# Adjacency pieces loaded on a third DMA queue (GpSimd's), with the start of the four-layer graph kernel rearranged

## The reference

```python
x = _layernorm(x + L0(x, adj, W, b))
x = _layernorm(x + L1(x, t, adj, B, W1, b1, W2, b2))
x = _layernorm(x + L2(x, adj, weight, bias))
x = _layernorm(x + L3(x, adj, kernel, bias))
# L0: relu([X, (adj @ X + X) / (degree + 1)] @ W + b), rows scaled to length 1
# L1: tanh([X, t] @ W1 + b1) @ W2 + b2 + adj @ XB - degree * XB,  XB = X @ B.T
# L2: per row the last 100 neighbours, weighted by powers of 0.5 (a cumulative
#     count along the row gives each one's place), times (X @ weight), + bias
# L3: adj @ expmap(X), then logmap, @ kernel + bias
```

## Time and profile before

| what | us |
|---|---|
| median of three runs (169.04 to 169.3) | 169.18 |
| the profiled execution | 167.48 |
| its span, first to last instruction | 165.2 |
| PE, DVE, ACT, POOL busy | 128.9, 107.6, 69.5, 42.8 |
| granted TensorE clock, mean over the span | 0.968 |

### The profile page before, as it was taken

One profiled execution on the slowest core, in us unless ns is written; L12 is line 12 of the kernel. 1 busy time (PEld: TensorE's weight loads), 2 busy tenths in 40 slices (PEclk: granted clock), 3 DMA queues, 4 the chain that ended last, 5 costly groups with the idle time before them and its releaser, 6 DMA issues.

```text
span 165.2 us, 2074 instructions
## 1 busy us (share of the span) xinstructions
PE 128.9 (78%) x728; PEld 67.7 (41%) x728; DVE 107.6 (65%) x240; ACT 69.5 (42%) x138; POOL 42.8 (26%) x50
## 2 busy tenths in 40 slices
PE   0018869957998899899999899999999899992000
PEld 0007753511443245143533555677447644572000
DVE  0589987789999999995176110622623888538861
ACT  0034201448566666754378547512113320257440
POOL 0000000102430143114344000433412552713290
PEclk9999999999999999999999999999999999999755
DMA  6999999999999995000000000000000000000006
GB/s 131 257 304 350 318 300 354 272 206 287 346 347 255 289 215 124 0 0 0 4 0 0 0 0 0 4 0 0 0 4 0 0 2 0 0 4 0 0 0 127
DMA packets 13945, 18.59 MB, mean 112 GB/s; under 512 B 5360, under 2 KB 5616, under 8 KB 13936
## 3 DMA queue, kind: packets, MB, share of 16 engines
q1 hardware_dynamic: 7728, 9.68, 22.2%
q10 hardware_dynamic: 6208, 8.78, 19.2%
HBM read 17.93 MB, written 0.52 MB: 112 GB/s over the span
## 4 chain that ended last, share of the span: by engine, by line
PE 45%; DVE 25%; DMA 13%; POOL 5%; issue 4%; ACT 4%; POOLq 1%; ACTq 0%; DVEq 0%
PE psS L737 15%; DMA WT<-adj 10%; PE psN L737 5%; PE psC L737 5%; DVE AT L494 4%; DVE AT L495 4%; DMA X<-x 3%; PE psC L804 3%; PE psC L806 3%; PE psX L813 2%; POOL root L272 2%; POOL nroot L291 2%; ACT WT L365 2%; PE psX L763 1%; PE psH L783 1%
## 5 line engine op out<-in xcount | busy, mean ns | idle before, releaser
L365 ACT ACTIVATE WT<-psC 128x512 int16<-128x512 f32 x64 | 36.9, 596 | 13.0 <-PE psC L806 9.8
L737 PE MATMUL psS<-AT,XP 128*128 128x512 bf16 x128 | 35.0, 390 | 0.9 <-DVE XP L500 0.9
L272 POOL TENSOR_TENSOR root<-var,power 128x4 f32<-128x4 f32 (+1 forms) x16 | 18.7, 1170 | 44.2 <-DVE var L546 19.5
L804 PE MATMUL psC<-AT,cb 128*128 128x512 bf16 x56 | 21.4, 383 | 4.5 <-ACT WT L365 4.5
L806 PE MATMUL psC<-AT,cb 128*128 128x512 bf16 x64 | 24.2, 379 | 0.0
L737 PEld LDWEIGHTS psS<-AT,XP 128*128 128x128 f16 x128 | 11.9, 100 | 17.0 <-issue 3.7
L763 PE MATMUL psX<-cb,XP 128*128 128x128 bf16 x32 | 4.0, 264 | 12.7 <-DVE XP L632 11.9
L494 DVE STREAM_TRANSPOSE AT<-stage 128x1024 bf16<-128x1024 bf16 x10 | 13.2, 1318 | 0.8 <-DMA stage<-adj 0.7
L804 PEld LDWEIGHTS psC<-AT,cb 128*128 128x128 bf16 x56 | 5.6, 101 | 18.6 <-ACT WT L365 16.0
L495 DVE STREAM_TRANSPOSE AT<-stage 128x1024 bf16<-128x1024 bf16 x10 | 12.7, 1270 | 0.0
L285 POOL TENSOR_TENSOR XB<-X,weights 128x256 f32<-128x256 f32 x12 | 9.6, 808 | 9.6 <-DVE X L551 9.6
(11 more groups left out here) (143 smaller groups left out, 223.3 us busy)
## 6 DMA issues: line engine op xcount, KB each, us to landing
stage<-adj ACTq DMA_DIRECT2D x20, 256.0 KB, 11.3
stage<-adj SPq DMA_DIRECT2D x20, 256.0 KB, 12.3
WT<-adj SPq DMA_DIRECT2D x12, 256.0 KB, 14.7
WT<-adj ACTq DMA_DIRECT2D x12, 256.0 KB, 14.0
out<-X SPq DMA_DIRECT2D x6, 64.0 KB, 1.9
weights<-weights_packed SPq DMA_DIRECT2D x1, 353.5 KB, 15.8
X<-x SPq DMA_DIRECT2D x2, 128.0 KB, 3.1
X<-x ACTq DMA_DIRECT2D x2, 128.0 KB, 4.0
```

The costliest lines, as they stand in the source:

```text
L272: nc.gpsimd.tensor_tensor(root[:, e, 0:n], var[:, e, 0:n], power[:, 0:n, 0:NR], ALU.pow).then_inc(root_ready, 1)
L365: nc.scalar.activation(WT[:, e, chain_block(bank, k)], psC[bank][:], ACT.Relu).then_inc(chain_taken, 1)
L737: ins = nc.tensor.matmul(bank, XP[:, l % 2, c], matrix, start=(c == 0), stop=last)
L804: nc.tensor.matmul(acc, C("past"), AT[:, c + 1, e], start=False, stop=False, skip_group_check=True)
```

## The change

X was loaded ahead of piece 0; now piece 0 comes first on both queues. DVE transposes it before it looks at X. The high half of layer 0's `XP` is made by ACT (`split_high`), and so is the copy of the own parts (`take_z`); POOL adds the bias (`add_bias`). The own parts get a PSUM bank each (`z_bank`). PE counts and sums chunk 0 in two halves (`count_half`, `sum_half`), the first after pieces 0 and 1, and makes the own parts between the halves. The upper quarters of pieces 8 to 15 are issued by POOL's queue, with semaphores of their own. DVE's orders, the chain's and layer 1's are rewritten. The core of the diff:

```diff
-        CHAIN_IN_SUMS = (0, 11, 27, 42)
-        CHAIN_LOOP = 56
+        CHAIN_IN_SUMS = (0, 10, 27, 38)
+        CHAIN_LOOP = 46
+        def chain_in_sums(e):
+            return range(CHAIN_IN_SUMS[e], min(CHAIN_IN_SUMS[e] + NB // 2, NB * e))
+        def chain_after_sums(e):
+            return range(chain_in_sums(e).stop, CHAIN_IN_SUMS[e + 1])
...
# sync: load_lower(0), X, constants, own weights, load_lower(1..3), weights, load_lower(4..15)
# gpsimd
+            def load_upper(m):
+                pool.wait_ge(transposed, m - 8 + 1 if m < 12 else m - 6 + 1)
+                for q in range(NQ // 2, NQ):
+                    nc.gpsimd.dma_start(slot(slot_of(m))[QD * q:QD * (q + 1)], ad[m, q]
+                                        ).then_inc(pool_filled[slot_of(m)], 16)
+            def add_bias(e):
+                pool.wait_ge(z_taken, e + 1)
+                nc.gpsimd.tensor_tensor(Z[:, chunk(e)], Z[:, chunk(e)], per_feature(W("b0")), ALU.add
+                                        ).then_inc(z_biased, 1)
...
+            pool.wait_ge(own_weights_loaded, 16)
+            for e in range(NE):
+                load_upper(ALL_SLOTS + e)
+                add_bias(e)
             pool.wait_ge(consts_loaded, 16)
-            for e in range(NE - 1):
+            for e in range(NE - 2):
                 weigh(e)
-                if e >= 1:
-                    residual(1, e - 1)
+                if e == 0:
+                    load_upper(12)
                 l2_root(e)
+                if e == 0:
+                    load_upper(13)
                 var_root(0, e)
                 diagonals(e)
+                if e == 0:
+                    load_upper(14)
+                    load_upper(15)
...
# scalar
+            def split_high():
+                act.wait_ge(inverse_ready, 1)
+                nc.scalar.activation(XP[:, 0, :, 0:D], X[:], ACT.Copy, scale=xs[:, 4:5]).then_inc(high_ready, 1)
+            load_upper(0)
             for q in range(NQ // 2, NQ):
                 act.dma_start(X[QD * q:QD * (q + 1)], xd[q]).then_inc(x_loaded, 16)
-            for m in range(NR):
+            for m in range(1, 6):
                 load_upper(m)
+            split_high()
+            take_xt(0, 0)
+            load_upper(6)
+            take_xt(0, 1)
+            load_upper(7)
+            take_z(0)
+            take_xt(0, 2)
+            take_z(1)
+            take_xt(0, 3)
+            take_z(2)
+            take_z(3)
...
# vector
+            transposes(0)
             # x_loaded; largest value and mean of X
+            transposes(1)
             # scale, inverse; XB; low half of XP
+            for m in range(2, 6):
+                transposes(m)
+            take_degrees(0)
+            transposes(6)
+            activate0(0)
+            transposes(7)
+            combine0(0)
+            transposes(8)
+            normalise(0, 0)
+            transposes(9)
+            take_degrees(1)
+            transposes(10)
+            activate0(1)
+            transposes(11)
+            combine0(1)
+            transposes(12)
+            normalise(0, 1)
+            take_degrees(2)
+            transposes(13)
+            transposes(14)
+            transposes(15)
+            activate0(2)
...
# tensor
             pe.wait_ge(consts_loaded, 16)
+            count_half(0)
             transpose_x(0, 0)
+            sum_half(0)
+            transpose_x(0, 1)
+            own_part(0)
+            transpose_x(0, 2)
+            own_part(1)
+            transpose_x(0, 3)
+            own_part(2)
+            own_part(3)
+            count_half(1)
+            sum_half(1)
...
+                    if e == 1 and 2 <= k < 10:
+                        sum_block(1, k % 2, (k - 2) // 2)
+                    if n == 2 * NB + 3:
+                        transpose_x(1, 0)
+                    if n == 2 * NB + 5:
+                        hidden(0)
...
# after layer 0's last sums: links 38 to 45 with dense(0, 3), transpose_x(1, 1), hidden(1), 8 blocks
+            for c in range(2 * NR):
+                sum_block(1, 2, c)
+            for o in range(3):
+                sums(1, o, range(2, 3))
             sums(1, 0, late)
             add_own(1, 0)
+            chain_pair(CHAIN_LOOP)
...
+            dense(1, 2)
+            chain_pair(CHAIN_LOOP + 12)
             hidden(3)
-            dense(1, 2)
-            sums(1, 3, range(2, 4))
+            chain_pair(CHAIN_LOOP + 14)
+            chain_pair(CHAIN_LOOP + 16)
+            sums(1, 3, range(0, 4))
             add_own(1, 3)
```

More of the change, by code:

```diff
@@ L118, in gnn_kernel @@
         filled = [sem(f"filled{i}") for i in range(ALL_SLOTS)]
+        pool_filled = [sem(f"pool_filled{i}") for i in range(ALL_SLOTS)]
         transposed = sem("transposed")
@@ L234, in load_lower @@
                                  ).then_inc(filled[slot_of(m)], 16)
+            first = WR["WB"][0]
+            load_lower(0)
             for q in range(NQ // 2):
@@ L411, in _ @@
                 if e >= 1 and e < 3:
-                    for n in range(CHAIN_IN_SUMS[e], NB * e):
+                    for n in chain_in_sums(e):
                         take_chain(n)
@@ L501, in split @@
                                                ALU.mult, ALU.subtract).then_inc(parts_ready, 1)
-            def take_z(e):
-                dve.wait_ge(z_ready, e + 1)
-                rows = psN[e % 2][:, 0:NR * D].rearrange("p (r f) -> p r f", r=NR)
-                nc.vector.tensor_tensor(Z[:, chunk(e)], rows, per_feature(W("b0")), ALU.add).then_inc(z_taken, 1)
             def take_degrees(e):
@@ L650, in _ @@
                                            bundle, ALU.mult, ALU.add).then_inc(centred, 1)
-            for e in range(NE - 1):
-                transposes(NR * e + 4)
-                if e >= 1:
-                    normalise(0, e - 1)
-                take_degrees(e)
-                transposes(NR * e + 5)
-                transposes(NR * e + 6)
-                activate0(e)
-                transposes(NR * e + 7)
-                combine0(e)
-            normalise(0, NE - 2)
-            take_degrees(NE - 1)
-            activate0(NE - 1)
-            combine0(NE - 1)
-            normalise(0, NE - 1)
+            take_degrees(3)
+            combine0(2)
+            activate0(3)
+            normalise(0, 2)
+            combine0(3)
+            normalise(0, 3)
             add_residual(1, 0)
@@ L785, in counts, with count_half, sum_half @@
                 ins.then_inc(counts_ready, 1)
+            def count_half(h):
+                cols = slice(2 * P * h, 2 * P * (h + 1))
+                pe.wait_ge(transposed, 2 * h + 2)
+                for k in range(NR):
+                    for g in range(NQ):
+                        ins = nc.tensor.matmul(psH[QD * g:QD * (g + 1), cols], C("count"), AT[:, NQ * g + k, 0, cols],
+                                               start=(k == 0), stop=(k == NR - 1))
+                if h == 1:
+                    ins.then_inc(counts_ready, 1)
+            def sum_half(h):
+                cols = slice(2 * P * h, 2 * P * (h + 1))
+                for c in range(NB):
+                    nc.tensor.matmul(psS[0][:, cols], XP[:, 0, c], AT[:, c, 0, cols], start=(c == 0), stop=False)
+                    if h == 1 and c == NB // 2 - 1:
+                        degrees(0)
+                for r in range(2 * h, 2 * h + 2):
+                    ins = nc.tensor.matmul(psS[0][:, P * r:P * (r + 1)], XP[:, 0, r], C("paired"), start=False,
+                                           stop=(r % 2 == 1))
+                if h == 1:
+                    ins.then_inc(sum_ready, 1)
             def degrees(e):
```

174 lines of the change are left out of this document (88 added, 86 removed).

## The result

The changed kernel takes 174.0 us (median of four runs, 172.21 to 174.9). The kernel before took 169.24 us beside it, so the ratio is 1.027, with an interval of 1.020 to 1.034: slower, as forecast, but by 4.8 us and not by 1.4, and outside the range. The profiled execution took 173.4 us, its span is 171.6, the mean clock 0.947.

The account below looks back on a forecast made before the run. Loads lead until piece 6, then DVE, then PE from chunk 3's counts to `dense(2, 0)`, then a latency tail. Loads alone 0.8 us slower, degrees at low clock 2.9; between them 1.4 slower, 170.6 us, range 167.5 to 172.4.

Parts of the forecast that it names:

- Piece 9 follows behind `add_bias(0)` at 28 to 29 us and takes up to 0.5 us more: Loads before piece 6: POOL's next issue after piece 8 adds 0.2 to 0.5 us to piece 8's 1.5 us delay.
- T: Start of piece 6's transposes on DVE, 33.49 us before; by the loads forecast at 35.2 to 35.5 us.
- The ceiling: Loads: three queues move no more than two, 355 GB/s, so piece 8's 0.52 MB delays every later piece by 1.5 us.
- What sets T: the degrees: `take_degrees(0)` ahead of piece 6 waits for degrees at about 36.3 us at PE's low clock, making T about 36.7.
- its own alternative: If the half sums already raise PE's clock, the degrees are there by 32 us and the loads set T.
- Piece 15 is done at T + 36.4: DVE from piece 6 to piece 15: 39.5 us before, less 2.65 for the moved `activate0(2)` and 0.45 of idle time.
- From chunk 3's counts on: PE until `dense(2, 0)`: 47.6 us as before, plus 3.7 of moved work and 2.2 of new waits.
- The chain's waits: PE before the last layer-1 sums: 1.8 us waiting for ACT's bank plus about 0.4 at links 54 to 57, together 2.2.
- The 15 us of the prediction: `normalise(0, 3)` comes about 15 us after piece 15, with PE having some 16 us of work, so its old gap goes.
- (1): Rival: the third queue costs early pieces nothing and degrees are in time; about 167.8 us, chance 0.28.
- (2): Rival: POOL's issues take 2.2 us each, delaying `weigh(1)` 2.2 us and `var_root(0, 0)` 1.2; 173 us, chance 0.12.
- (3): Rival: T near 34.4, saved 2.65 and 3.2 us pay for 3.7 and 2.2 exactly; 169.2 us, chance 0.1.

Follow-up runs that it names:

- the third experiment: Changed kernel with all 16 links of the chain's first chunk made before chunk 1's counts instead of 10; 173.11 us, ratio 1.019.
- the version meant to be the best: Changed kernel with upper quarters on ScalarE's queue, X first, pairs spread, weights loaded later, piece 6's transposes ahead of first degrees, centring moved; 168.46 us, ratio 1.000.
- the fourth experiment: Kernel before, with only the upper quarters of pieces 8 to 15 issued by GpSimd, each as its buffer is free; 179.56 us, ratio 1.058.
- the first: Changed kernel with the upper quarters of pieces 8 to 15 back on ScalarE's queue; 167.77 us, ratio 0.987.
- the second experiment: Changed kernel with GpSimd's issues for pieces 8 to 11 held back until piece 5 is transposed; 171.39 us, ratio 1.017.
- the one that takes each harm away: Changed kernel, GpSimd's queue kept, issues held until piece 5 is transposed, scaling ahead of pieces 10 and 11, 16 links before chunk 1's counts; 168.38 us, ratio 0.995.
- its siblings: Changed kernel with upper quarters on ScalarE's queue: alone 167.77 us, with the chain's pairs spread 167.37, with X first and pairs spread 167.77.

## Why the prediction was wrong

**The step that failed: "Piece 9 follows behind `add_bias(0)` at 28 to 29 us and takes up to 0.5 us more".** The loads' share of T was reckoned as 0.52 MB of piece 8 and at most 0.17 MB of piece 9. But the four `add_bias` come one behind the other, 0.73 us each, with an issue between: pieces 9, 10 and 11 go out at 29.00, 31.00 and 32.77, and pieces 5 and 6 were still under way. In the trace's packets, the third queue moved 1.31 MB before T. At the prediction's own 0.35 MB for each us that is 3.7 us; T is later by 4.3 than before, and by 4.1 than with ScalarE's queue (33.70). The two parts can be told apart at piece 4, whose transposes wait for data in both: 29.85 against 27.98. So piece 8 cost 1.9 us where 1.5 were forecast, and pieces 9 to 11, whose first packet moved at 33.3, the other 2.2 where 0.2 to 0.5 were forecast. These sizes are of one execution each: T was 39.76 in the third experiment, whose start is that of the changed kernel, and 33.70 to 34.95 in the four profiles with ScalarE's queue and this order of DVE. The mechanism, a shared ceiling at which a third queue only takes from the others, was right, and its size was off by a factor of two, mostly for want of counting what the queue issues before T. On ACT the same transfers stand behind pieces 6 and 7 in one queue and can't overtake.

**The ceiling** was taken to stay at 355 GB/s. With the third queue it fell: 294 and 280 GB/s in the two stretches from 18 to 22 us, where ScalarE's queue had 359 and 307, and 288 and 295 from 34 to 38, where it had 332 and 342. Not all of the low rates are the third queue's. From 22 to 24 us it moved nothing, and the rate was 284, with ScalarE's queue 278, in the kernel before 282. The weights' second load stands in SP's queue about then in all three, and in the version meant to be the best the low rates went with it to 30 to 34 us. I put the 0.4 to 0.6 us beyond the 3.7 down to the lower ceiling; that is argued and not shown, and in the fourth experiment, where the bytes give 6.0 of 10.9 us, the same account leaves nearly half open.

**Equal turns.** The queues between 18 and 20 us (packets, MB, share of 16 engines):

```profile
q0 software_dynamic: 77, 0.27, 48.1%
q1 hardware_dynamic: 86, 0.16, 28.9%
q10 hardware_dynamic: 88, 0.16, 28.6%
```

Without the small ones these are 66 packets of POOL's queue, 77 of SP's and 78 of ACT's, but POOL's are of 4096 B and the others' of 2048: 0.27, 0.16 and 0.16 MB. Between 36 and 38 us it is 92 packets against 101. The Trainium skill ("DMA: Bandwidth & Descriptors", section "Queues, rings and completion order") says that an engine takes turns between queues by packets, where a packet of the page may hold several descriptors and need not be one of the trace's; the counts agree with turns of equal number. So a third queue with double packets takes nearly half and not a third. No run could make its packets smaller, and that their size sets the share is read from counts, not shown by an experiment.

**"What sets T: the degrees"** was wrong, as its own alternative said. The half sums at 22.29 still run at the slow pace, 0.226 us for 256 columns, the first own parts take 1.47, the next 1.06, where they took 1.92 before, though the granted clock reads 1.00 from 14 us on in all stretches until 44. PE has made the degrees by 32.75 us, and DVE takes them at 35.22. I had averaged this case with that of the loads; its value (36.7) was close to the T that came, for another reason.

**"Piece 15 is done at T + 36.4"** holds to 0.2 us where DVE does not wait: T + 36.2, 36.3 in the first and the third experiment, and T + 40.8 and T + 37.6 in two others, where the waits of 4.40 and 1.06 us make up the rest. What the prediction missed is that PE runs dry. Chunk 0's sums hold ten links instead of eleven before the next counts and no other work, so with T 4.3 us late PE idles 4.56 us, its clock falls to half, chunk 1's counts and sums are slow, and DVE waits 1.84 us for `dense(0, 1)`. A late transfer was paid for twice. It is a term that only exists when piece 7 is late, by T as here or by `weigh(0)` as in the second experiment; with T at 33.70 and no such wait the idle time was 0.53 us and the clock stayed.

**From chunk 3's counts on**, 54.3 us against 53.5. The chain's waits were 0.41 + 0.40 + 0.78 = 1.6 instead of 2.2; the old gap before `parts(1, 3)` did not go but grew to 0.83 us; the work itself was 0.6 longer than summed. `normalise(0, 3)` comes 93.86 - 76.16 = 17.7 us after the counts, not 15. The 15 us of the prediction were read from PE's counts, which before began 3.2 us behind piece 15, and were then used from piece 15: from there it was 91.6 - 72.95 = 18.7 us before and is 17.8 now. Part of it are DVE's long instructions. The kernel after, DVE in that stretch:

```profile
76.75 0.43 DVE L581 TENSOR_TENSOR u<-y 128x256 f32<-128x256 f32 x1
...
84.11 1.28 DVE L581 TENSOR_TENSOR u<-y 128x256 f32<-128x256 f32 x1
...
93.03 0.83 DVE L564 SCALAR_TENSOR_TENSOR XP<-X,XP 128x256 f16<-128x256 f32 x1
```

L581 takes 0.43 us at 76.75 and 1.28 at 84.11. With ScalarE's queue it is 1.27 as well, and POOL is computing beside it (a `diag` of 1.04 us starts 0.05 us earlier), so it is not the queue. The Trainium skill ("SBUF — State Buffer", section "Who interferes with whom") has a VectorE instruction with two SBUF inputs contend with GpSimd's reads; the rows agree, POOL being idle at 76.75.

**The rivals.** (1), the third queue free, is refuted by the first and the fourth experiment. (2), long issues: they cost 0.55 to 0.73 us, below the 1.1 taken, but what it describes, `weigh` queued behind issues, is real as soon as many stand together (2.65 us in the second experiment). The Trainium skill's warning ("SBUF — State Buffer", section "Who interferes with whom"), cited ahead, that descriptors starve beside DVE did not show: two issues take 1.09 us while DVE transposes; whether the transposes use both ports no run shows. (3), cancelling: with T at 33.70 the moved parts do more than cancel, they gain 1.3%. The break-even at T = 34.4 rested on the first profile of before, which is at the fast end.

**What is shown.** That the queue costs 6.2 us is shown by undoing it; the early transfers by the second and the fourth experiment and by the one that takes each harm away; PE's idle time and clock by the third beside the first. How the delay ahead of T divides between bytes, rate and turns stays open. The best kernel measured is that with X first and the upper quarters on ScalarE's queue, 167.18 us; its siblings (167.37 to 167.77) can't be told from it.

## What to carry to other kernels

A new queue is not only more bandwidth but a way to overtake: list in MB what it issues before the next due transfer and divide by the rate at the ceiling for the least that it costs (3.7 us of 4.3 here, 6.0 of 10.9 in the fourth experiment), or keep such transfers in line behind the urgent ones. Where a bound moves later, ask at once which engine runs dry, for how long, and whether its clock falls, and place work there that does not depend on the late data.

## What the runs showed of the hardware

One hardware queue alone moved 204 to 229 GB/s, two 328 to 367 in most stretches and 270 to 307 while the weights' second load (353.5 KB) was under way, SP's with POOL's 293 to 298, and all three 280 to 294 in the changed kernel from 18 to 22 us. POOL's issue of a DMA took 0.54 to 0.73 us, for 256 KB as for 64 KB.

From the begin of an issue to the first packet of data of a queue that stood empty it took 4.3 to 6.8 us on POOL's (13.58 to 18.06 and 29.00 to 33.34 in the changed kernel, 33.10 to 39.91 in the second experiment), and no less on ACT's (31.78 to 38.08 in the kernel before, 22.35 to 27.82 in the version meant to be the best), with the other queues busy. In these five cases a queue that had run empty stood idle for that long, whoever issued.

POOL's packets hold 4096 B, whether the rows of 2 KB lie side by side, alternate, or belong to different partitions, where those of SP's and ACT's queues hold 2048 B.
